# Group tags applied inside TensorE's sum, and a fence that sets non-neighbours apart, in a graph kernel on Trainium2

## The chip, the cores and the metric

The kernel runs on one core of one Trainium2 chip. The metric is the device time of one execution in microseconds (us). Before the change it is 3187.29 us, the median of 3 runs (3184.47 to 3189.19). Engines are named as in the profile: PE is TensorE's matmul, PEld its weight load, DVE is VectorE, ACT is ScalarE, POOL is GpSimd, SP is SyncE.

## The reference, cut to what matters

There are B = 16 graphs of N = 512 nodes with C = 64 features. Four graph layers follow each other; the change touches only the first. For every node it thins the neighbourhood, then takes three weighted quantiles of every feature over the neighbours that are left:

```python
neigh = (adj_ > 0) & ~eye
rank = jnp.cumsum(ni, axis=-1) - ni                 # the how-manieth neighbour of its row
nb = ni.sum(-1)
skip = jnp.maximum(jnp.where(nb > T, (nb + K - 1) // K, 1), 1)      # T, K = 10, 2
rem = neigh & (sk > 1) & (rank % sk == sk - 1) & mask[:, :, None]
rem = rem | jnp.swapaxes(rem, 1, 2)
adj_d = jnp.where(rem, 0.0, adj_)
s = jnp.sort(jnp.where(nd[..., None], x[:, None, :, :], jnp.inf), axis=2)
for tau, w in zip((0.25, 0.5, 0.75), (0.25, 0.5, 0.25)):
    pos = tau * jnp.maximum(nv - 1, 0); lo, hi = floor(pos), ceil(pos)
    agg += w * (s[lo] + (pos - lo) * (s[hi] - s[lo]))
```

The output is a layer norm of x plus the last layer, shape (16, 512, 64), float32.

## The kernel before, in words

**Staging.** At the start DVE makes tables in `stage`, SP stores them to memory (`consts_d`) and loads them back later as `consts`. All features of all graphs are then sorted at once by a network of comparisons on DVE; its swaps are replayed to give every node its rank in each feature. Graph 0's preparation is laid into this replay. Then comes the main loop over 16 graphs, and after it a loop for the last three layers that the change does not touch.

**The main loop is a pipeline of three graphs.** In one round, graph `b` is selected (`select`) and turned into indices (`bits_*` on DVE), graph `b + 1` (called `p` in `region`) is prepared, graph `l = b - 1` is looked up in `units` (48 units; in each, PE spreads indices into `bcast`, ACT makes `hot` of them, PE multiplies `hot` with a table into `rows`, ACT evicts `rows` into `prod`, PE adds up in `found_bank`), and graph `d = b - 2` runs its dense part. The order of all this on PE, ACT and DVE is written out by hand: the same `select` and `region` stand once per engine, with `units(l, STEP[n])` between the other pieces, so each engine works through its own list in order and waits on semaphores.

**Preparation of graph p**, in order: ACT converts the adjacency (`adj_b`), PE turns it, ACT keeps it (`neigh_t`), SP stores it; DVE waits for that store and clears the diagonal (`clear_own`, L1424); PE counts neighbours (L584); DVE works out for each node the place of its dropped neighbours (`middles`: `s1`, `s2`); PE counts up along each row with an upper triangle of ones (`count_up`, L594); ACT takes the distance from the middle (`apart_from`, L1001, `apart_of`); DVE compares with `s2` and multiplies by the adjacency (`drop`, L1445); PE adds both directions (`both_ways`, L604 to L607); ACT and DVE finish `kept_t`.

**Selection of graph b** goes over 4 tiles of 128 nodes. PE multiplies the kept adjacency with `member` in 8 chunks of 512 columns (`chunk`, L624): chunks 0 and 1 are counts, 2 to 5 two sets of bit words, 6 and 7 the plane `first` from which the first neighbour of the next group is read. ACT evicts them (L1046). DVE's `select(b, i, l)` then marks where each quantile's group starts (L1496) and what lies below (L1498), makes differences of words (L1501), masks the exponent of `first` (L1504), multiplies it by a tag that holds the group's number (L1505, `first_at`) and multiplies the starts by it (L1508). PE sums the result over 15 groups with the identity as weights (`sum_first`, L748). `tile_read` tells ACT after L1505 that words and `first` may be overwritten.

## Time and profile before

| | |
|---|---|
| median of 3 runs | 3187.29 us (3184.47 to 3189.19) |
| the profiled execution | 3195.59 us, of which span 3193.8 us |
| DVE busy | 2805.5 us, 88% |
| PE busy / weight loads | 2251.2 us, 70% / 1000.7 us, 31% |
| ACT busy | 1991.7 us, 62% |
| sort and replay | to about 520 us |
| main loop | about 520 to 2860 us |
| last layers | to the end |

Busy time is the time in which an engine has an instruction in work. Matmuls overlap, so a busy PE is not one at its peak, and a matmul's own duration is longer than the step to the next one: eight L594 matmuls take 1.19 us in the chain, though each has a duration of 0.2 to 0.4 us. The same holds on DVE to a smaller degree, where the next instruction starts some 0.08 us before the end of the last. PEclk is the granted clock of TensorE as a share of 2.4 GHz; it stands at 1.2 or at 2.4 GHz, and a share in a window is the mean of the two.

### The profile page before, as it was taken

What the parts mean: (1) busy time and instruction counts of PE and PEld (TensorE: products, weight loads), DVE (VectorE), ACT (ScalarE), POOL (GpSimd) and SP (SyncE); (2) the same over time, 40 slices, a digit from 0 to 9 for tenths busy, and PEclk for the clock granted to TensorE, in tenths of its full rate; (3) what the DMA queues carried; (4) which work ended last, traced back from release to release, by engine and by line L of the source; (5) the groups of instructions that cost most, each with busy time, mean ns of one, the idle gap of its engine ahead of it and who ended that gap; (6) DMA issues with size and microseconds to landing.
All of it is one profiled execution on the core that took longest, in us unless ns stands there. A gap on an engine that the chain in (4) does not pass through costs nothing.

```text
span 3193.8 us, 45583 instructions
## 1 busy us (share of the span) xinstructions
PE 2251.2 (70%) x16081; PEld 1000.7 (31%) x16234; DVE 2805.5 (88%) x5398; ACT 1991.7 (62%) x3077; POOL 12.4 (0%) x24
## 2 busy tenths in 40 slices
PE   0000014387888988888888988888898889776996
PEld 0000002232333333333333333333333333224674
DVE  7999998998999989899999999999898999545776
ACT  2111443278787887778788877878788877741322
POOL 0000000000000000000000000000000000000000
PEclk6555557688998989899999989899898989886777
DMA  3001000000101001010100101010100100000101
GB/s 68 0 0 26 31 0 0 22 24 11 37 8 34 13 29 33 10 33 12 36 11 31 21 21 33 12 37 9 32 15 27 34 10 19 10 20 27 40 26 40
DMA packets 126915, 72.05 MB, mean 23 GB/s; under 512 B 95512, under 2 KB 110058, under 8 KB 126698
## 3 DMA queue, kind: packets, MB, share of 16 engines
q1 hardware_dynamic: 122570, 68.23, 8.3%
q8 instruction: 121, 1.98, 0.3%
q10 hardware_dynamic: 4128, 1.05, 0.2%
q14 instruction: 96, 0.79, 0.1%
HBM read 41.05 MB, written 15.58 MB: 18 GB/s over the span
## 4 chain that ended last, share of the span: by engine, by line
PE 44%; DVE 32%; ACT 13%; issue 7%; SPq 2%; DMA 1%; DVEq 0%; ACTq 0%
PE ring L624 10%; PE rows L665 8%; ACT hot L1078 6%; PE bcast L637 5%; PE found_bank L677 5%; DVE keys L1326 3%; DVE keys L1327 3%; PE bcast L748 2%; PE bcast L757 2%; PE bank L919 2%; ACT prod L1071 2%; DVE picked L1524 2%; DVE delta L1367 2%; DVE delta L1365 1%; DVE perm L1369 1%
## 5 line engine op out<-in xcount | busy, mean ns | idle before, releaser
L1078 ACT ACTIVATE hot<-bcast,consts 128x1024 f16<-128x1024 f32 x744 | 830.7, 1117 | 136.0 <-PE bcast L637 135.5
L665 PE MATMUL rows<-hot,table 128*64 128x512 f16 x3072 | 525.7, 423 | 0.0
L624 PE MATMUL ring<-member,neigh_t 128*128 128x512 bf16 x1925 | 488.9, 392 | 40.0 <-issue 15.1
L1071 ACT ACTIVATE prod<-rows 128x512 f32<-128x512 f32 x720 | 431.1, 599 | 10.4 <-PE rows L665 10.4
L637 PE MATMUL bcast<-idx_t,consts 32*128 32x512 f16 x1488 | 311.3, 415 | 159.6 <-ACT hot L1078 158.0
L654 PE MATMUL rows<-fine_rows,consts 32*128 32x512 bf16 x768 | 316.3, 412 | 18.8 <-DMA fine_rows<-turned 18.1
L562 PE MATMUL ring<-identb,adj_b 128*128 128x128 bf16 x256 | 33.1, 258 | 368.9 <-ACT adj_b L974 357.6
L624 PEld LDWEIGHTS ring<-member,neigh_t 128*128 128x128 bf16 x2048 | 187.4, 101 | 318.8 <-issue 100.2
L677 PE MATMUL found_bank<-prod,consts 128*32 128x512 f32 x1536 | 240.2, 702 | 11.3 <-ACT prod L1071 10.5
L637 PEld LDWEIGHTS bcast<-idx_t,consts 32*128 32x128 f16 x1488 | 70.8, 92 | 499.0 <-ACT hot L1078 332.2
L1524 DVE TENSOR_TENSOR picked<-picked 128x3072 uint16<-128x3072 uint16 (+2 forms) x192 | 209.5, 1091 | 11.2
L1046 ACT ACTIVATE words<-ring 128x512 uint16<-128x512 f32 x256 | 153.4, 600 | 97.9 <-PE ring L624 79.4
L665 PEld LDWEIGHTS rows<-hot,table 128*64 128x64 f16 x3072 | 115.1, 112 | 190.6 <-issue 186.6
L968 ACT ACTIVATE keys<-keys 128x1024 f32<-128x1024 f32 (+7 forms) x72 | 35.5, 544 | 216.2 <-DVE keys L1327 216.2
L562 PEld LDWEIGHTS ring<-identb,adj_b 128*128 128x128 bf16 x256 | 19.6, 111 | 406.1 <-issue 332.7
L1014 ACT ACTIVATE swap<-swapped 128x2048 f16<-128x2048 uint8 (+8 forms) x45 | 73.8, 1643 | 111.5 <-DVE delta L1367 105.1
L1046 ACT ACTIVATE late<-ring 128x512 bf16<-128x512 f32 x128 | 76.9, 601 | 75.4 <-PE ring L624 73.3
L1516 DVE TENSOR_TENSOR picked<-below,words 128x2880 f16<-128x2880 bf16 x64 | 106.1, 1658 | 7.2
L1415 DVE TENSOR_TENSOR member<-words,shares 128x3072 bf16<-128x3072 bf16 x64 | 112.0, 1751 | 0.0
L1490 DVE TENSOR_TENSOR picked<-below,late 128x3072 uint16<-128x3072 bf16 x64 | 112.0, 1751 | 0.0
L1518 DVE TENSOR_TENSOR picked<-below,late 128x3072 uint16<-128x3072 bf16 x64 | 112.0, 1750 | 0.0
L1508 DVE TENSOR_TENSOR picked<-picked,first_at 128x2880 bf16<-128x2880 bf16 x64 | 106.1, 1658 | 2.2
(347 smaller groups left out, 4326.8 us busy)
## 6 DMA issues: line engine op xcount, KB each, us to landing
late<-in_adj_dram SPq DMA_DIRECT2D x16, 1024.0 KB, 5.4
adjt_d<-neigh_t SPq DMA_DIRECT2D x16, 512.0 KB, 2.7
fine_rows<-turned SPq DMA_DIRECT2D x512, 8.0 KB
fine_rows<-turned SPq DMA_DIRECT2D x512, 16.0 KB
turned<-adjt_d SPq DMA_DIRECT2D x16, 512.0 KB, 3.5
adj_s<-adjt_d SPq DMA_DIRECT2D x16, 512.0 KB, 3.8
xt_d<-keys SPq DMA_DIRECT2D x2, 1024.0 KB, 10.5
parts_d<-parts SPq DMA_DIRECT2D x4, 512.0 KB, 6.9
```

The lines of the kernel that those rows point to most:

```text
L624: ins = mm(ring[u % 2][:, :], kept_t[:, j, P * i:P * i + P], member[:, j, n // 2, 512 * (n % 2):512 * (n % 2) + 512], start=(j == 0), stop ...
L637: ins = mm(to[:, h, :], sel_a[r:r + 32, at:at + P], idx_t[r:r + 32, k, :], start=True, stop=True, tile_position=(r, 0))
L654: mm(rows[u % 2][:, :], sel_f[r:r + 32, :], fine_rows[r:r + 32, 2 * k + ROW_SLOT[g8], :], start=True, stop=False, tile_position=(r, 0), sk ...
L665: ins = mm(rows[u % 2][C * h:C * h + C, :], table[:, s, GROUPS * h + g8, :], hot[:, u % HOT, h, :], start=False, stop=(s == 1), skip_group ...
L677: mm(found_bank[to:to + 32, :], sum_to[:, g8 % 4, :], prod[:, u % DEEP, :], start=(m == 0), stop=(u >= UNITS - 4), skip_group_check=True). ...
L1046: run(dst, ring[u % 2][:, :], ACT.Copy).then_inc(S["cw_ev"], 1)
L1071: run(prod[:, u % DEEP, :], rows[u % 2][:, :], ACT.Relu).then_inc(S["prod_by_act"], 1)
L1078: run(hot[:, u % HOT].rearrange(flat), spread_bank(l, u)[0][:, 0:2, :].rearrange(flat), ACT.Relu, bias=eq_bias[:, :]).then_inc(S["hot_read ...
L1415: tt(member[:, j, 1:4, :].rearrange("p s (g c) -> p s g c", g=G), own[:, :, :].unsqueeze(1).to_broadcast([P, 3, G, C]), shares[:, :, j, :] ...
L1490: did(tt(picked[:, w], below[:, :], change[:, w, :].unsqueeze(1).to_broadcast([P, TAUS, G * C]), ALU.mult))
L1518: tt(picked[:, 2], below[:, :, :], change[:, 2, :].unsqueeze(1).to_broadcast([P, TAUS, G * C]), ALU.mult).then_inc(S["mask_used"], 1)
L1524: then(tt(a[:, :, 0:n], a[:, :, 0:n], a[:, :, n:2 * n], ALU.bitwise_xor))
```

## The change

Five things are done. (1) The 15 group tags no longer go into `first_at` on DVE; they are the weights of PE's sum: `tagged` holds 15 identities of 128 x 128, each scaled by its tag. L1505 goes, and L1508 reads the plane `first` itself. (2) ACT's leave to overwrite is told in two parts: `words_read` after the words are read, and `first_picked`, after L1508, for `first`. (3) In `count_up` a matmul of `adj_b` with `fence` (an identity times 4096) opens each of the 4 sums, so that neighbours carry 4096 more than non-neighbours; `s1` takes it off again. (4) `drop` is then one comparison with one scalar, without the product with `adj_b`. (5) At the start DVE makes `fence`, `tags` and `tagged`; the table `consts` grows by 448 columns of 4 bytes; one memset on POOL goes.

```diff
-FIELDS = (... ("group_id", 512, F16), ("first_tag", 512, BF16), 
+FIELDS = (... ("group_id", 512, F16), ("tagged", (G - 1) * 64, BF16),
...
             def count_up(b, i):
...
+                mm(ring[i % 2][:, :], fence[:, :], adj_b[:, i, :], start=True, stop=False)
                 for j in range(NT):
-                    ins = mm(ring[i % 2][:, P * j:N], neigh_t[:, j, P * i:P * i + P], upper[:, 0:N - P * j], start=(j == 0), stop=(j == NT - 1))
+                    ins = mm(ring[i % 2][:, P * j:N], neigh_t[:, j, P * i:P * i + P], upper[:, 0:N - P * j], start=False, stop=(j == NT - 1))
...
                 for g in range(G - 1):
-                    ins = mm(first_sum.rearrange("p (k c) -> p k c", k=TAUS), identb[:, :], plane[:, :, C * g:C * g + C], start=(g == 0), stop=(g == G - 2),
+                    ins = mm(first_sum.rearrange("p (k c) -> p k c", k=TAUS), tagged[:, g, :], plane[:, :, C * g:C * g + C], start=(g == 0), stop=(g == G - 2),
...
                 if n == 0:
-                    wait(act, S["tile_read"], NT * b + i - 1)
                     wait(act, S["cnt_read"], NT * b + i - 1)
                 if n == 2:
-                    wait(act, S["tile_read"], NT * b + i)
+                    wait(act, S["words_read"], NT * b + i)
+                if n == 6:
+                    wait(act, S["first_picked"], NT * b + i)
...
+            did(ts(fence[:, :], ident[:, :], FENCE, None, ALU.mult))
...
-            did(ts(made_of["first_tag"], made_of["group_id"], 1.0 / 32, 1.0 + 2.0 / 32, ALU.mult, ALU.add))
+            then(ts(tags, made_of["group_id"], 1.0 / 32, 1.0 + 2.0 / 32, ALU.mult, ALU.add))
+            did(tt(made_of["tagged"].rearrange("p (g n) -> p g n", n=P), ident[:, :].unsqueeze(1).to_broadcast([P, G - 1, P]),
+                   tags.rearrange("p (g c) -> p g c", c=C)[:, 1:, 0:1].to_broadcast([P, G - 1, P]), ALU.mult))
...
-                then(ts(s1, f1, -1.0, 1.0, ALU.mult, ALU.add))
+                then(ts(s1, f1, -1.0, 1.0 - FENCE, ALU.mult, ALU.add))
...
                 dve.wait_ge(S["apart_ready"], NT * b + i + 1)
-                stt(out=drop1[:, i, :], in0=apart_of[:, i % 2, :], scalar=s2[:, i:i + 1], in1=adj_b[:, i, :], op0=ALU.is_equal, op1=ALU.mult).then_inc(S["drop_ready"], 1)
+                ts(drop1[:, i, :], apart_of[:, i % 2, :], s2[:, i:i + 1], None, ALU.is_equal).then_inc(S["drop_ready"], 1)
...
-                did(v.tensor_copy(change[:, 1:3, last:], words[:, 1:3, 0:C]))
+                v.tensor_copy(change[:, 1:3, last:], words[:, 1:3, 0:C]).then_inc(S["words_read"], 1)
                 dve.wait_ge(S["cw_ev"], NT * CW * b + CW * i + CW)
                 then(ts(first[:, :].bitcast(U16), first[:, :].bitcast(U16), FIRST, None, ALU.bitwise_and))
-                tt(first_at[:, 0:last], first[:, C:], first_tag[:, 1:, :].rearrange(flat), ALU.mult).then_inc(S["tile_read"], 1)
-                dve.wait_ge(S["tile_read"], NT * b + i + 1)
-                need(count[0])
-                tt(starts[:, :, 0:last], starts[:, :, 0:last], first_at[:, 0:last].unsqueeze(1).to_broadcast([P, TAUS, last]), ALU.mult).then_inc(S["first_picked"], 1)
+                tt(starts[:, :, 0:last], starts[:, :, 0:last], first[:, C:].unsqueeze(1).to_broadcast([P, TAUS, last]), ALU.mult).then_inc(S["first_picked"], 1)
```

Here is PE in the main loop, at the first two of the four `count_up` of a graph; L637, L654 and L665 are one unit of the lookup. First before, then the changed kernel, whose line numbers are 2 higher from there on:

```order
L637 MATMUL bcast<-idx_t,consts 128x512 x2
L654 MATMUL rows<-fine_rows,consts 128x512
L665 MATMUL rows<-hot,table 64x512 x4
L594 MATMUL ring<-consts,neigh_t 128x512
L594 MATMUL ring<-consts,neigh_t 128x384
L594 MATMUL ring<-consts,neigh_t 128x256
L594 MATMUL ring<-consts,neigh_t 128x128
```

```order
L639 MATMUL bcast<-idx_t,consts 128x512 x2
L656 MATMUL rows<-fine_rows,consts 128x512
L667 MATMUL rows<-hot,table 64x512 x4
L594 MATMUL ring<-adj_b,fence 128x512
L596 MATMUL ring<-consts,neigh_t 128x512
L596 MATMUL ring<-consts,neigh_t 128x384
L596 MATMUL ring<-consts,neigh_t 128x256
L596 MATMUL ring<-consts,neigh_t 128x128
```

One matmul of 512 columns more stands in front of every count; nothing else moves on PE.

The second place is DVE in the selection of a tile, before and changed (L1504 is L1510 there, L1508 is L1511):

```order
L1502 COPY late<-words 128x2x64
L1504 TENSOR_SCALAR late<-late 128x1024 [waits cw_ev]
L1505 TENSOR_TENSOR first_at<-late,consts 128x960 [waits dve_chain]
L1508 TENSOR_TENSOR picked<-picked,first_at 128x3x960 [waits dve_chain,tile_read]
L1509 TENSOR_SCALAR words<-cnt 128x960
```

```order
L1508 COPY late<-words 128x2x64
L1510 TENSOR_SCALAR late<-late 128x1024 [waits cw_ev]
L1511 TENSOR_TENSOR picked<-picked,late 128x3x960 [waits dve_chain]
L1512 TENSOR_SCALAR words<-cnt 128x960
```

One instruction is gone per tile. The third place is ACT, at the eviction of the 8 chunks of a tile (cnt, words, late), before and changed:

```order
L1046 ACTIVATE cnt<-ring 128x512 [waits cw_ps,cnt_read,tile_read]
L1046 ACTIVATE cnt<-ring 128x512 [waits cw_ps]
L1046 ACTIVATE words<-ring 128x512 [waits cw_ps,tile_read]
L1046 ACTIVATE words<-ring 128x512 [waits cw_ps] x3
L1046 ACTIVATE late<-ring 128x512 [waits cw_ps] x2
```

```order
L1049 ACTIVATE cnt<-ring 128x512 [waits cw_ps,cnt_read]
L1049 ACTIVATE cnt<-ring 128x512 [waits cw_ps]
L1049 ACTIVATE words<-ring 128x512 [waits cw_ps,words_read]
L1049 ACTIVATE words<-ring 128x512 [waits cw_ps] x3
L1049 ACTIVATE late<-ring 128x512 [waits cw_ps,first_picked]
L1049 ACTIVATE late<-ring 128x512 [waits cw_ps]
```

The wait of the words comes loose from `first`, and the first `late` has a wait of its own.

## Rows read from the trace of the kernel before

**Rows 1.** The page: busy time of each engine, and the chain that ended last.

```profile
PE 2251.2 (70%) x16081; PEld 1000.7 (31%) x16234; DVE 2805.5 (88%) x5398; ACT 1991.7 (62%) x3077; POOL 12.4 (0%) x24
PE 44%; DVE 32%; ACT 13%; issue 7%; SPq 2%; DMA 1%; DVEq 0%; ACTq 0%
```

**Rows 2.** Timeline of DVE: start, us, clearing of the diagonal, idle before and releaser.

```profile
875.98 0.63 DVE L1424 TENSOR_TENSOR neigh_t<-neigh_t,identb 128x128 bf16<-128x128 bf16 x4 [1.39 <-DMA adjt_d<-neigh_t]
...
1304.03 0.63 DVE L1424 TENSOR_TENSOR neigh_t<-neigh_t,identb 128x128 bf16<-128x128 bf16 x4 [4.19 <-DMA adjt_d<-neigh_t]
...
1585.39 0.63 DVE L1424 TENSOR_TENSOR neigh_t<-neigh_t,identb 128x128 bf16<-128x128 bf16 x4
...
2577.20 0.63 DVE L1424 TENSOR_TENSOR neigh_t<-neigh_t,identb 128x128 bf16<-128x128 bf16 x4 [0.60 <-DMA adjt_d<-neigh_t]
```

**Rows 3.** Windows, one graph each: engines busy, PEclk, DMA share, GB/s.

```profile
1158.80:1304.00 145.20, 127.36 (x886) 51.78 (x896) 130.82 (x265) 113.26 (x179) 0.00 (x0) 0.88 0.09 23
1304.00:1445.40 141.40, 122.61 (x886) 49.73 (x896) 130.94 (x265) 112.95 (x179) 0.00 (x0) 0.91 0.09 23
1585.40:1725.00 139.60, 120.03 (x886) 49.30 (x896) 130.88 (x266) 113.04 (x178) 0.00 (x0) 0.93 0.09 24
```

**Rows 4.** Timeline of DVE in the selection of one tile.

```profile
1243.93 1.23 DVE L1496 TENSOR_SCALAR picked<-cnt,above 128x960 bf16<-128x960 f16 x3
1245.07 1.22 DVE L1498 TENSOR_SCALAR below<-cnt,limit 128x960 bf16<-128x960 f16 x3
...
1248.03 0.66 DVE L1505 TENSOR_TENSOR first_at<-late,consts 128x960 bf16<-128x960 bf16 x1
1248.72 1.66 DVE L1508 TENSOR_TENSOR picked<-picked,first_at 128x2880 bf16<-128x2880 bf16 x1
```

**Rows 5.** Timeline of DVE around the four drops of one graph.

```profile
1316.22 1.42 DVE L1445 SCALAR_TENSOR_TENSOR adj_b<-apart_of,small,adj_b 128x512 bf16<-128x512 f16 x2
1317.55 0.68 DVE L1412 TENSOR_TENSOR words<-group_of,consts 128x1024 bf16<-128x1024 f16 x1
...
1321.92 1.42 DVE L1445 SCALAR_TENSOR_TENSOR adj_b<-apart_of,small,adj_b 128x512 bf16<-128x512 f16 x2 [1.42 <-ACT apart_of L1001]
```

**Rows 6.** The chain in the same stretch: start, us, what.

```profile
1316.27 1.19 PE ring L594 x8
...
1321.31 0.59 ACT apart_of L1001
...
1321.92 1.43 DVE adj_b L1445 x2
...
1323.69 0.38 PE ring L605
```

**Rows 7.** Timeline of PE in the same stretch, behind the last drop.

```profile
1323.69 0.38 PE L605 MATMUL ring<-adj_b,minus 128*128 128x512 bf16 x1 [0.73 <-DVE adj_b L1445]
```

**Rows 8.** Timeline of ACT: lookups around the counts, and the second pair of distances.

```profile
1311.06 1.11 ACT L1078 ACTIVATE hot<-bcast,consts 128x1024 f16<-128x1024 f32 x1 [1.68 <-PE bcast L637]
...
1317.83 1.11 ACT L1078 ACTIVATE hot<-bcast,consts 128x1024 f16<-128x1024 f32 x1 [0.47 <-PE bcast L637]
...
1321.19 1.27 ACT L1001 ACTIVATE apart_of<-ring,small 128x512 f16<-128x512 f32 x2
```

**Rows 9.** The chain in the replay, the first round, and two later selections.

```profile
418.67 0.75 DVE adj_b L1445
...
428.10 0.74 DVE adj_b L1445
...
541.35 0.67 DVE first_at L1505
...
615.64 1.42 DVE adj_b L1445 x2
...
619.93 1.32 DVE adj_b L1445 x2
...
1500.51 0.67 DVE first_at L1505
...
1829.42 0.67 DVE first_at L1505
```

**Rows 10.** Timelines of DVE and SP at the start, and the DMA issues.

```profile
19.78 2.29 DVE L1325 TENSOR_TENSOR swapped<-keys 128x2048 uint8<-128x2048 f32 x1 [8.07 <-ACT keys L954]
...
33.39 2.29 DVE L1325 TENSOR_TENSOR swapped<-keys 128x2048 uint8<-128x2048 f32 x1 [6.91 <-DMA xt_d<-keys]
...
19.64 0.42 SPq L376 DMA_DIRECT2D consts_d<-parts  x1
20.10 2.07 SPq L379 DMA_DIRECT2D xt_d<-keys  x2
...
xt_d<-keys SPq DMA_DIRECT2D x2, 1024.0 KB, 10.5
consts_d<-parts SPq DMA_DIRECT2D x1, 881.0 KB, 3.8
```

**Rows 11.** Waits in total: engine, line, waited for, us, times, longest.

```profile
PEld bcast L748 <- DVE picked L1508: 14.0, 8, 10.0
```

More of the change, by code:

```diff
@@ L35 @@
 FIRST, TAG = 0x7F80, 0x7C
+FENCE = 4096.0
 DEEP = 6
@@ L47 @@
 TURN_ORDER = (K, 0, K + 1, K + 2, 1, 2, 3, 4, 5)
-FIELDS = (("sel_a", 256, F16), ("upper", 256, BF16), ("group_id", 512, F16), ("first_tag", 512, BF16),
+FIELDS = (("sel_a", 256, F16), ("upper", 256, BF16), ("group_id", 512, F16), ("tagged", (G - 1) * 64, BF16),
           ("sum_to", 4 * 32, F32), ("one_u", 32, U16), ("ones_b", 1, BF16), ("sel_f", 64, BF16), ("eq_bias", 1, F32))
@@ L161, in build @@
         minus = sb("minus", [P, P], BF16)
+        fence = sb("fence", [P, P], BF16)
         rowsum = sb("rowsum", [P, B, NT], F32)
@@ L227, in build @@
             at_f = stage[:, 4104:4112]
+            tags = stage[:, 4608:5120].bitcast(BF16)
             column, shift = delta[:, 0:512], swap[:, 0, 0:512]
@@ L242, in build @@
         upper, sel_a, sel_f, one_u, eq_bias = (views[n] for n in ("upper", "sel_a", "sel_f", "one_u", "eq_bias"))
-        group_id, first_tag = (views[n].rearrange("p (g c) -> p g c", c=C) for n in ("group_id", "first_tag"))
+        group_id, tagged = (views[n].rearrange("p (g c) -> p g c", c=w) for n, w in (("group_id", C), ("tagged", P)))
         sum_to = views["sum_to"].rearrange("p (g c) -> p g c", c=32)
@@ L251, in build @@
         adj_f = late[:, :, :].rearrange("p a n -> p (a n)").bitcast(F32).rearrange("p (t n) -> p t n", t=NT)
-        first_at = sb("first_at", [P, G * C], BF16)
         adj_b = sb("adj_b", [P, NT, N], BF16)
@@ L331, in build @@
             first_picked size_picked sums_ps sums_ev perm_made twos_done stage_ready stage_out consts_in neighT_ready nb_ps middle_ready apart_ready cnt_ps drop_ready rs_ps kept_made kept_ready nv_ps nv_read member_ready cw_ps cw_ev
-            tile_read cnt_read mask_used idx_ready idxT_ps idxT_ev table_in adjl_in bc_ps place_ps
-            odd_in later_in hot_ready row_ps prod_by_act prod_by_dve found_ps nb_read sum_ev xt_out span_ready unspan_clear unspan_in x_t_in x1T_ps x1T_ev gcn_ev h_ps h_ev y_ps z_ready
+            cnt_read mask_used idx_ready idxT_ps idxT_ev table_in adjl_in bc_ps place_ps
+            odd_in later_in words_read hot_ready row_ps prod_by_act prod_by_dve found_ps nb_read sum_ev xt_out span_ready unspan_clear unspan_in x_t_in x1T_ps x1T_ev gcn_ev h_ps h_ev y_ps z_ready
             sd_ready x1_ready tr_ps split_ready g_ps dve_chain out_done sp_passed pe_passed w23_ready wT_ps
@@ L509, in _ @@
             made(g.memset(below[:, :, (G - 1) * C:], 1.0))
-            made(g.memset(first_at[:, (G - 1) * C:], 0.0))
             made(g.memset(table[:, :, :, :], 0.0))
```

## The prediction

> **What bounds the kernel now.** I first read the page's busy times and its chain. DVE is busy 88% of the span, PE 70%, ACT 62%; but the chain that ended last lies 44% on PE and only 32% on DVE [rows 1], and much of DVE's share is the sort and its replay before 520 us. So DVE is the fullest engine and yet not clearly the one that sets the pace. Next I read the timeline of DVE at one fixed place of each round, the clearing of the diagonal: where DVE comes to it early, it waits for the store of the adjacency, which hangs on PE and ACT; where it comes late, it does not wait. Of the 14 clearings from 737 us on, 11 come with a wait of 0.3 to 4.2 us and 3 with none [rows 2]. From 876.0 to 2577.2 us lie 12 rounds, 141.8 us each on average [rows 2]. Then the windows of single rounds: DVE's busy time is 130.8 or 130.9 us in every round, whether the round takes 139.6, 141.4 or 145.2 us; what goes with the length is the granted clock, 0.93, 0.91, 0.88, and with it PE's busy time, 120.0, 122.6, 127.4 us [rows 3]. A round is thus paced by the PE-ACT loop, with DVE only 0 to 4 us behind it. The chain says the same: followed through the main loop, the 14 rounds from 660 us on have first_at on it 15 times out of 56 (first at 932 us, in four rounds, last at 1829.42) [rows 9]; elsewhere it runs over PE and ACT, touching DVE mainly at the clearing and at the second pair of drops, which is on it in every round [rows 6].
>
> How near the two are: by the clock shares, a round has 25.4 us at 1.2 GHz at 0.91 and 34.8 us at 0.88 (twice the missing share times the length), and 3.8 us more of length, 0.40 us for each us. From the 141.4 us round down to 0.93 (19.5 us) that gives 139.1 us for the PE-ACT loop alone, where DVE-paced rounds take 139.6 [rows 3]. The two ways differ by 0.5 us in 140.
>
> **The change part by part.**
>
> *first_at goes.* L1505 starts at 1248.03 and L1508 at 1248.72: 0.69 us per tile [rows 4], 64 tiles, 44 us of DVE. Where it is on the path: in the first selection, which has no lookups beside it, all 4 times [rows 9], so 4 x 0.69 = 2.8 us gained. In later rounds DVE merely reaches the clearing 2.8 us sooner and waits there longer; that wait is what is late next. What it can give there stands under "pacing" below.
>
> *The drop as one comparison.* Two old drops follow each other from 1316.22 to 1317.55, 0.665 us apiece [rows 5]. The new one is a comparison with one scalar like L1496, three of which (960 columns, float16 to bfloat16) take 1.14 us from start to start, 0.38 each [rows 4]. Bounds for 512 columns: 0.20 (by columns alone) and 0.38 (no cheaper than 960). I take 0.26, since most of the duration goes with the columns; the gain is 0.40 us each (0.28 to 0.46), 26 us of DVE in all. On the path: the 4 in the replay, where the chain is all DVE, and the 4 of the first round [rows 9]: 8 x 0.40 = 3.2 us. In the 14 later rounds the second pair is on the chain, but only half of it can be gained: its first drop starts at 1321.92 while the ACT pair that feeds both runs from 1321.19 to 1322.46 [rows 8]. The second drop cannot start before about 1322.55, so the pair ends at 1322.91 instead of 1323.34: 0.43 us. PE has waited 0.73 us for it [rows 7], so it can take it. 14 x 0.43 = 6.0 us.
>
> *The fence.* Four matmuls of 512 columns per graph. Eight L594 matmuls (two tiles, 2560 columns) took 1.19 us in the chain at the full clock [rows 6], 0.24 us per 512 columns; at 1.2 GHz twice that is the upper bound, zero the lower, where PE would have waited. PE is behind here, not ahead: ACT waits 1.68 us for PE's spread just before the first pair of counts and 0.47 us just after the second [rows 8], and both pairs are on the chain. So I take 0.24 x 4 = 0.95 us per round at full price, 14 rounds: +13.3 us. In the replay and the first round DVE is the path and the fence is free. Its weight load is hidden as those of the other counts are.
>
> *Tags as weights.* The 15 matmuls of a sum keep their number and size and had a weight load each before; only which weights changes. Nothing. Multiplying by `first` in place of `first_at` is the same form: nothing.
>
> *ACT's waits.* Words may be overwritten sooner. The new wait stands before chunk 6: behind it on ACT are the rest of the tile's evictions and the units, and PE waits for both. L1508 ends at 1250.4 us [rows 4]; ACT came to chunk 6 of the next tile about 7 us later. Nothing in the main loop. If this cover went, each of 60 tiles would pay up to the 1.66 us of L1508.
>
> *The start.* DVE makes `tagged`, 1920 columns of float32 with two tensors, at most the 2.29 us of a float32 operation of 2048 columns, and `fence`; it then waited 8.07 us for ACT, which hides both [rows 10]. The table is 224 KB longer. It is stored just ahead of the 2048 KB whose landing DVE waits for until 33.39 us, 6.91 us [rows 10]: 2929 KB from 19.64 us to there are 213 KB per us, so 1.05 us later (0 if the engines had room). I take +1.0.
>
> *Pacing.* Four rounds were wholly or partly paced by DVE. Freed from it they fall back to the PE-ACT loop, 0.5 us shorter each: 2 us. PE's weight loads waited 14.0 us for L1508 in 8 places, 10.0 of it in one at the start [rows 11]; the other 4.0 us, each under the 0.69 us by which L1508 comes sooner, would go. I count half, as PE had other work at hand in some: 2 us.
>
> *The sum.* -2.8 - 3.2 + 1.0 = -5.0 us before the first lookups; then -6.0 + 13.3 - 2 - 2 = +3.3 us. Together -1.7 us, on the profiled execution's 3195.6 us (span 3193.8 and 1.8 around it). That execution is 8 us above the median 3187.3; I take the difference as the same in both kernels, and the forecast is 3185.6, say 3186 us.
>
> The page says DVE is at 88%, and the Trainium skill ("Perfetto Trace Analysis", Identifying the Most-Contended Engine) says to take the engine of highest occupancy as the one to speed up first. By that rule the 70 us taken off DVE should come out almost whole. It is my first rival; the windows speak against it.
>
> **The rivals.**
>
> *A: DVE is the pace after all.* If every round followed DVE, it would give back 4 x (0.69 + 0.40) = 4.4 us: 15 rounds and the replay, 66 us, less the 1.0 of the start: about 3122 us. For it: 88%, and three clearings without a wait. Against it: equal DVE work in rounds 6 us apart in length [rows 3], and 11 clearings that waited. A milder form: half of it, 3155. Chance of both 0.12.
>
> *B: the clock gets better.* The rounds of 141.4 and 145.2 us have 6 to 15 us more at 1.2 GHz than those of 139.6 [rows 3]. The counts and PE's shorter wait for the drops make PE a little fuller. If with that every round came out like the best, the 12 rounds would average 139.1 + 0.95 - 0.43 = 139.6 in place of 141.8: 14 x 2.2 = 31 us, less the pacing gain already in it; with -5, 3154 us. Half of it is likelier: 3168. For it: three rounds in a row held 0.93. Against it: the low stretches lie where PE waits for the adjacency and at the turn of the rounds, not at the counts. Chance 0.20.
>
> *C: slower.* The fence is the only work added to the loop that sets the pace, and it moves every later piece of the round. DVE's pace of 139.6 us held four rounds steady at 0.93; with DVE early, nothing holds them, and they may fall to 0.91 like their neighbours. Place: the rounds from 1445 to 1865 us and the one at 907. Price: 4 x (141.4 - 139.6) = 7 us, and one further round in four going to 0.88, 3 x 3.8 = 11 us: 3186 + 18 = 3204 us. It decides from the point at which the freed rounds show 0.91 or less. For it: PE-paced rounds are the longer ones in this trace. Chance 0.20.
>
> *D: the change buys DVE less than it says* (the comparison runs no faster than the product, 0.66 us). Then -3.2 and -6.0 go: 3195 us. Against it: the form L1496. Chance 0.03.
>
> **How the numbers follow.** The forecast has 0.45, with 3179 to 3193 as its own range. Of measurement: within 0.2% (6.4 us, 3180.9 to 3193.7) nothing can be told from no change. Faster: all of A, 0.17 of B's 0.20 and 0.06 of the forecast's: 0.35. Slower: 0.17 of C, 0.02 of D, 0.03 of the forecast: 0.22. The rest, 0.43, is no change. The range of 8 in 10 goes down to B's milder form and a little beyond, and up to C: 3160 to 3203. It takes in the fence at nothing (-13) and at double (+13).
>
> **What would show it.** After the change: no L1505; drops of 0.26 us from start to start; DVE busy about 2735 us; the wait at the clearing longer by 2.5 to 3 us in most rounds and present in all; PE's wait before L605 shorter by about 0.4 us or a new one of DVE on ACT between the drops of the second pair; rounds of PE-paced length 0.5 us up at the same clock; the first lookups (about 650 us) 5 us sooner; DVE's share of the chain below 25%. The forecast is wrong if the rounds shorten by more than 2 us with an unchanged clock (A), or if the mean clock of the rounds moves by more than 0.01 (B or C).

## The result and the profile after

| | before | after |
|---|---|---|
| median (lowest to highest), 8 runs each | 3188.11 us (3184.47 to 3192.8) | 3198.93 us (3194.62 to 3205.38) |
| ratio | | 1.0028, 95% interval 1.0018 to 1.0039 |
| the profiled execution, its span | 3195.59 us, 3193.8 us | 3198.18 us, 3196.4 us |

The changed kernel is slower by 0.28%, some 9 us (the two medians are 10.8 us apart). The forecast was no change (3186 us, 1.7 us faster) with a range of 3160 to 3203; the time lies in the range, the sign was wrong. The first place to look is again the page, busy time and chain, of the changed kernel (before: [rows 1]):

```profile
PE 2270.3 (71%) x16145; PEld 1008.6 (32%) x16298; DVE 2741.5 (86%) x5336; ACT 1990.4 (62%) x3077; POOL 12.3 (0%) x23
PE 52%; DVE 21%; ACT 16%; issue 7%; SPq 2%; DMA 2%; DVEq 0%; ACTq 0%
```

DVE lost 64 us of work and 62 instructions, PE gained 64 matmuls and 19 us. DVE's share of the chain fell from 32% to 21%, and what it gave up went to PE. The clearing of the diagonal is the marker of the rounds; here it is in the changed kernel, on the timeline of DVE (start, duration, at the end the idle time before it and what ended that):

```profile
603.83 0.63 DVE L1430 TENSOR_TENSOR neigh_t<-neigh_t,identb 128x128 bf16<-128x128 bf16 x4
...
729.79 0.63 DVE L1430 TENSOR_TENSOR neigh_t<-neigh_t,identb 128x128 bf16<-128x128 bf16 x4 [0.25 <-DMA adjt_d<-neigh_t]
...
867.41 0.63 DVE L1430 TENSOR_TENSOR neigh_t<-neigh_t,identb 128x128 bf16<-128x128 bf16 x4 [2.87 <-DMA adjt_d<-neigh_t]
...
1295.78 0.63 DVE L1430 TENSOR_TENSOR neigh_t<-neigh_t,identb 128x128 bf16<-128x128 bf16 x4 [7.50 <-DMA adjt_d<-neigh_t]
...
1863.65 0.63 DVE L1430 TENSOR_TENSOR neigh_t<-neigh_t,identb 128x128 bf16<-128x128 bf16 x4 [2.30 <-DMA adjt_d<-neigh_t]
...
2579.81 0.63 DVE L1430 TENSOR_TENSOR neigh_t<-neigh_t,identb 128x128 bf16<-128x128 bf16 x4 [2.72 <-DMA adjt_d<-neigh_t]
```

The same places before, as far as [rows 2] do not have them:

```profile
607.46 0.63 DVE L1424 TENSOR_TENSOR neigh_t<-neigh_t,identb 128x128 bf16<-128x128 bf16 x4
...
737.02 0.63 DVE L1424 TENSOR_TENSOR neigh_t<-neigh_t,identb 128x128 bf16<-128x128 bf16 x4 [0.99 <-DMA adjt_d<-neigh_t]
```

The changed kernel is 3.6 us ahead at the first of them, 7.2 at the second and 8.6 at the third (867.41 against 875.98 [rows 2]). From there 12 rounds take 1712.4 us in place of 1701.2; it loses 11.2 us and is 2.6 us behind at 2577, which is the whole difference of the spans. So there are two parts: a start that gains, and rounds that lose 0.93 us each. The windows of single rounds and of the 12 together, after (for the rounds before, [rows 3]):

```profile
1150.90:1296.30 145.40, 127.92 (x890) 52.17 (x900) 126.70 (x262) 112.94 (x178) 0.00 (x0) 0.88 0.09 23
1296.30:1438.20 141.90, 123.60 (x890) 50.15 (x900) 126.81 (x262) 112.97 (x178) 0.00 (x0) 0.91 0.09 23
1723.80:1864.20 140.40, 121.41 (x890) 49.62 (x900) 126.81 (x263) 112.94 (x178) 0.00 (x0) 0.93 0.10 24
867.90:2580.30 1712.40, 1489.19 (x10684) 605.93 (x10800) 1521.65 (x3134) 1357.33 (x2138) 0.00 (x0) 0.91 0.09 23
```

and the 12 rounds before, in the same columns:

```profile
876.00:2577.20 1701.20, 1473.67 (x10636) 599.41 (x10752) 1570.76 (x3181) 1358.31 (x2138) 0.00 (x0) 0.91 0.09 23
```

DVE has 4.1 us less work in every round, as forecast. Rounds at the same granted clock, 0.88, 0.91 and 0.93, take 145.4, 141.9 and 140.4 us where [rows 3] have 145.2, 141.4 and 139.6: a cost of 0.2 to 0.8 us at an unchanged clock. The last of these pairs sets a round paced by PE and ACT against one that DVE paced.

**One round followed on ACT.** The rounds that begin at 1304.0 (before) and 1295.8 (after) run at the same clock, so their events can be laid side by side. ACT's lookups and the pair of distances, after:

```profile
1302.93 1.11 ACT L1081 ACTIVATE hot<-bcast,consts 128x1024 f16<-128x1024 f32 x1 [1.80 <-PE bcast L639]
...
1306.50 1.11 ACT L1081 ACTIVATE hot<-bcast,consts 128x1024 f16<-128x1024 f32 x1 [0.67 <-PE bcast L639]
...
1310.61 1.11 ACT L1081 ACTIVATE hot<-bcast,consts 128x1024 f16<-128x1024 f32 x1 [0.90 <-PE bcast L639]
...
1313.97 1.27 ACT L1003 ACTIVATE apart_of<-ring,small 128x512 f16<-128x512 f32 x2
```

Counted from the clearing, the first of these comes 7.15 us in (before 1311.06 - 1304.03 = 7.03 [rows 2, 8]) and the third 14.83 us in (before 13.80 [rows 8]). Across the two pairs of counts ACT falls back from 0.12 to 1.03 us; its waits for PE's spread grew from 1.68 to 1.80 and from 0.47 to 0.90 us. After the last drop it is at 0.54, and so it stays to the end of the round. The forecast for this was +0.95 for four fences and -0.43 for the pair of drops, +0.52. The drops themselves, timeline of DVE:

```profile
1308.38 0.62 DVE L1451 TENSOR_SCALAR adj_b<-apart_of,small 128x512 bf16<-128x512 f16 x2
1308.91 0.69 DVE L1418 TENSOR_TENSOR words<-group_of,consts 128x1024 bf16<-128x1024 f16 x1
...
1314.69 0.35 DVE L1451 TENSOR_SCALAR adj_b<-apart_of,small 128x512 bf16<-128x512 f16 x1 [2.82 <-ACT apart_of L1003]
1315.27 0.35 DVE L1451 TENSOR_SCALAR adj_b<-apart_of,small 128x512 bf16<-128x512 f16 x1 [0.23 <-ACT apart_of L1003]
```

Two take 0.53 us, 0.265 each, against 0.665 [rows 5]. The second pair is now split by a wait for ACT of 0.23 us, and PE finds it ready (before, 0.73 us of wait for `adj_b` [rows 7]):

```profile
1304.18 0.38 PE L594 MATMUL ring<-adj_b,fence 128*128 128x512 bf16 x1
...
1315.98 0.38 PE L607 MATMUL ring<-adj_b,minus 128*128 128x512 bf16 x1 [0.25 <-issue]
```

What the chain of waits has at this place (start, us, what):

```profile
1308.62 0.32 PE ring L594
1308.94 0.54 PE ring L596 x4
1309.48 0.22 PE ring L594
1309.70 0.54 PE ring L596 x4
...
1314.08 1.16 ACT apart_of L1003 x2
...
1315.23 0.01 ACT hot L1081
```

The fence is two links of it, and the drops are no link any more ([rows 6] had them with 1.43 us). Over the 14 rounds from 737 us on, the chain has the fence 42 times, three of its four matmuls in every round, and a drop once, at 747.22. The waits in total (who, for what, us, times, longest) tell where DVE's saved time went:

```profile
DVE neigh_t L1430 <- DMA adjt_d<-neigh_t: 48.4, 14, 7.5
DVE adj_b L1451 <- ACT apart_of L1003: 43.4, 29, 4.8
```

Before they were 15.9 us in 11 places and 19.8 us in 14. Of the 64 us of work taken off DVE, 56 came back as these two waits.

### The profile page after: what moved, and what is told of

It is laid out like the page before. It is cut to its first block, busy times and chain, and to the rows that moved or that the text cites. A ratio compares the mean times of both kernels' runs of the same rounds, so it can differ in the third digit from the quotient of the medians.

```text
span 3196.4 us, 45647 instructions
## 1 busy us (share of the span) xinstructions
PE 2270.3 (71%) x16145; PEld 1008.6 (32%) x16298; DVE 2741.5 (86%) x5336; ACT 1990.4 (62%) x3077; POOL 12.3 (0%) x23
## 4 chain that ended last, share of the span: by engine, by line
PE 52%; DVE 21%; ACT 16%; issue 7%; SPq 2%; DMA 2%; DVEq 0%; ACTq 0%
PE ring L626 13%; PE rows L667 9%; ACT hot L1081 7%; PE bcast L639 6%; PE found_bank L679 6%; DVE keys L1332 3%; DVE keys L1333 3%; PE bcast L750 3%; PE bcast L759 2%; ACT prod L1074 2%; PE bank L921 2%; DVE delta L1373 2%; DVE delta L1371 1%; DVE perm L1375 1%; DVE perm L1376 1%
## 5 line engine op out<-in xcount | busy, mean ns | idle before, releaser
L1081 ACT ACTIVATE hot<-bcast,consts 128x1024 f16<-128x1024 f32 x744 | 830.8, 1117 | 143.6 <-PE bcast L639 143.3
L656 PE MATMUL rows<-fine_rows,consts 32*128 32x512 bf16 x768 | 316.4, 412 | 16.2 <-DMA fine_rows<-turned 15.9
L679 PE MATMUL found_bank<-prod,consts 128*32 128x512 f32 x1536 | 240.1, 702 | 11.2 <-ACT prod L1074 10.4
L1527 DVE TENSOR_TENSOR picked<-picked 128x3072 uint16<-128x3072 uint16 (+2 forms) x192 | 209.5, 1091 | 11.2
L1511 DVE TENSOR_TENSOR picked<-picked,late 128x2880 bf16<-128x2880 bf16 x64 | 106.1, 1658 | 2.2
```

The costliest lines, as they stand in the source:

```text
L656: mm(rows[u % 2][:, :], sel_f[r:r + 32, :], fine_rows[r:r + 32, 2 * k + ROW_SLOT[g8], :], start=True, stop=False, tile_position=(r, 0), sk ...
L679: mm(found_bank[to:to + 32, :], sum_to[:, g8 % 4, :], prod[:, u % DEEP, :], start=(m == 0), stop=(u >= UNITS - 4), skip_group_check=True). ...
L1081: run(hot[:, u % HOT].rearrange(flat), spread_bank(l, u)[0][:, 0:2, :].rearrange(flat), ACT.Relu, bias=eq_bias[:, :]).then_inc(S["hot_read ...
L1527: then(tt(a[:, :, 0:n], a[:, :, 0:n], a[:, :, n:2 * n], ALU.bitwise_xor))
```

## Experiments

Two theories were to be told apart. The first: the rounds are the PE-ACT loop, the change is a sum of small terms of work (fence dear, drops cheap, tags nothing), and DVE's work in the rounds is free. The second: the work matters little, and what moved is the granted clock, because rounds that DVE no longer paces fall to a lower one. Beside them stand the old rivals: the fence is hidden in waits of PE, and DVE is the pace.

One thing had to be settled first. Executions of one and the same kernel differ in their mean granted clock, and their time with it: of one comparison's runs of the kernel before, one had 0.820 and took 3184.9 us, another 0.811 and took 3209.5. Over the 161 executions of the first three comparisons whose clock is known, each taken against the mean of its kernel, the time falls by 2.2 us for each 0.001 of mean clock (2.24 over all 190). The table gives, beside the measured ratio, the mean time taken at 0.817 with this slope (in brackets 95%). That is an adjustment and not a measurement, and it cannot say whether a kernel itself causes its clock.

| kernel | comparison | ratio to before (95%) | median us (runs) | mean clock | at 0.817, us |
|---|---|---|---|---|---|
| before | 2nd, 3rd, 4th | | 3195.4 (35), 3193.6 (29), 3203.1 (9) | .8154, .8163, .8123 | 3193.2 (0.6) |
| after_again | 3rd | 1.0022 (1.0012 to 1.0032) | 3202.5 | .8149 | 3196.5 (1.2), with the first 8 |
| before_again | 3rd | 0.9996 (0.9986 to 1.0007) | 3193.07 (12) | .8170 | 3192.9 (1.1) |
| tags_only | 2nd | 0.9977 (0.9963 to 0.9991) | 3187.21 (12) | .8187 | 3191.4 (1.1) |
| fence_only | 2nd | 1.0009 (0.9995 to 1.0023) | 3200.39 (12) | .8161 | 3197.7 (1.1) |
| fence_mm_alone | 2nd | 1.0014 (0.9999 to 1.0029) | 3200.63 (12) | .8187 | 3205.3 (0.9) |
| free_fence | 2nd | 0.9973 (0.9955 to 0.9992) | 3187.48 (12) | .8153 | 3183.3 (1.1) |
| no_fence_mm | 3rd | 0.9982 (0.9969 to 0.9996) | 3187.45 (12) | .8149 | 3184.5 (1.7) |
| ballast | 3rd | 1.0060 (1.0044 to 1.0075) | 3210.57 (5) | .8160 | 3210.4 (1.3) |
| free_fence_again | 4th | 0.9960 (0.9947 to 0.9974) | 3190.03 (5) | .8134 | 3183.0 (1.5) |
| free_fence_alone | 4th | 0.9955 (0.9941 to 0.9968) | 3188.27 (5) | .8148 | 3183.0 (0.9) |
| ff_pad1 | 4th | 0.9947 (0.9933 to 0.9961) | 3186.40 (5) | .8178 | 3187.6 (1.2) |
| ff_pad2 | 4th | 0.9959 (0.9946 to 0.9973) | 3189.89 (5) | .8168 | 3189.5 (0.4) |

Ratios of different comparisons should be held against each other with care: the kernel before itself stood at 3188, 3195, 3194 and 3203 us in the four, the last two of them on the same chip.

### tags_only: the tags moved into the sum, counts and drops as before

```diff
 (to the changed kernel)
-                mm(ring[i % 2][:, :], fence[:, :], adj_b[:, i, :], start=True, stop=False)
-                then(ts(s1, f1, -1.0, 1.0 - FENCE, ALU.mult, ALU.add))
+                then(ts(s1, f1, -1.0, 1.0, ALU.mult, ALU.add))
-                ts(drop1[:, i, :], apart_of[:, i % 2, :], s2[:, i:i + 1], None, ALU.is_equal)
+                stt(out=drop1[:, i, :], in0=apart_of[:, i % 2, :], scalar=s2[:, i:i + 1], in1=adj_b[:, i, :], op0=ALU.is_equal, op1=ALU.mult)
```

> The tags go into the sum and the product on DVE goes, but the drops are made as before and there is no fence. Theory 1 (a round is paced by PE and ACT; work on their path counts, DVE's does not): -2.8 us in the first selection, +1.0 at the start, nothing per round: 3186 us, 2 below before. Theory 2 (DVE's pace held several rounds at a high granted clock, and whatever makes DVE early loses that): 5 us more, 3191 us, with fewer rounds of 139.6 to 140 us than before. Rival (DVE sets the pace after all): 44 us faster, 3145 us.

It is faster than before, by 0.23%. Of that only 1.8 us (3193.2 - 3191.4) is there at equal clock, though 44 us of DVE work are gone (64 x 0.69 us from start to start; its busy time fell by 38.5 us): DVE is not the pace. The windows of this kernel, the 12 rounds and one that DVE had paced before, with the clearings at both its ends:

```profile
872.10:2571.90 1699.80, 1474.63 (x10639) 597.22 (x10756) 1540.23 (x3133) 1357.52 (x2138) 0.00 (x0) 0.91 0.09 23
1580.40:1722.00 141.60, 122.72 (x886) 49.70 (x896) 128.45 (x263) 112.89 (x179) 0.00 (x0) 0.91 0.09 23
```

```profile
1580.29 0.63 DVE L1429 TENSOR_TENSOR neigh_t<-neigh_t,identb 128x128 bf16<-128x128 bf16 x4 [3.35 <-DMA adjt_d<-neigh_t]
...
1721.85 0.63 DVE L1429 TENSOR_TENSOR neigh_t<-neigh_t,identb 128x128 bf16<-128x128 bf16 x4 [2.94 <-DMA adjt_d<-neigh_t]
```

With DVE out of the way the round that took 139.6 us at 0.93 [rows 3] takes 141.6 at 0.91. That is what the second theory said of this round. But the rounds that were at 0.88 are gone too: all 12 lie between 141.3 and 142.1 us, their sum of 1699.8 us is near the 1701.2 of before, and the kernel's mean clock is the highest of all, 0.8187. So DVE's pace is not needed to keep the clock up over the whole run.

### fence_mm_alone: before, with four matmuls more per graph that add nothing

```diff
 (to the kernel before)
+                mm(ring[i % 2][:, :], fence[:, :], adj_b[:, i, :], start=True, stop=False)    # fence is all zeros
-                    ins = mm(ring[i % 2][:, P * j:N], ..., start=(j == 0), stop=(j == NT - 1))
+                    ins = mm(ring[i % 2][:, P * j:N], ..., start=False, stop=(j == NT - 1))
```

> The kernel before with 4 more matmuls of 512 columns per graph in front of the counts, of a zero matrix; DVE does exactly what it did. This prices the matmul. Theory 1: 14 x 0.95 = +13 us, 3201 us, a little less where DVE paced the round. Theory 2: the same or less, since DVE is no earlier. Rival (DVE sets the pace): nothing, 3188 us.

The ratio, 1.0014, says little: the interval reaches from 0.9999 to 1.0029. The kernel ran at 0.8187 where the kernel before had 0.8154. At equal clock it costs 3205.3 - 3193.2 = 12.1 us, where 13.3 were forecast.

### fence_only: before, with the fence and the one comparison

```diff
 (to fence_mm_alone)
-FENCE = 0.0
+FENCE = 4096.0
-                then(ts(s1, f1, -1.0, 1.0, ALU.mult, ALU.add))
+                then(ts(s1, f1, -1.0, 1.0 - FENCE, ALU.mult, ALU.add))
-                stt(out=drop1[:, i, :], ..., op0=ALU.is_equal, op1=ALU.mult)
+                ts(drop1[:, i, :], apart_of[:, i % 2, :], s2[:, i:i + 1], None, ALU.is_equal)
```

> The fence matmul and the drop as one comparison, tags as before. Theory 1: each of 14 rounds +0.95 us for the fence and -0.43 for the drops, -3.2 us before the first lookups: +4, 3192 us. Theory 2: 5 us on top, 3197 us. Rival (DVE sets the pace): 26 us of DVE saved, 3162 us.

Not told from before by its ratio (0.9995 to 1.0023). Against fence_mm_alone it is 7.6 us faster at equal clock: that is what the cheaper drops are worth. Against the changed kernel, which has the tags besides, it is 1.2 us slower, within the error of both.

### free_fence: the changed kernel with the fence in the triangle's diagonal

The triangle of ones already meets each node's own adjacency block in the count. If its diagonal holds 4096, every neighbour carries the fence and no matmul is needed.

```diff
 (to the changed kernel)
-                mm(ring[i % 2][:, :], fence[:, :], adj_b[:, i, :], start=True, stop=False)
-            did(ts(made_of["upper"], place[:, :], own_p, None, ALU.is_ge))
+            then(ts(made_of["upper"], place[:, :], own_p, None, ALU.is_ge))
+            did(stt(out=made_of["upper"][:, 0:P], in0=ident[:, :], scalar=FENCE, in1=made_of["upper"][:, 0:P], op0=ALU.mult, op1=ALU.max))
-                then(ts(s1, f1, -1.0, 1.0 - FENCE, ALU.mult, ALU.add))
+                then(ts(s1, f1, -1.0, 2.0 - FENCE, ALU.mult, ALU.add))
```

> The whole change, but the 4096 comes without a matmul: the diagonal of the triangle that count_up multiplies with is 4096 in place of 1, and s1 takes 4095 off. PE then does what it did before the change, DVE what it does after. Theory 1: the 13.3 us of the fence go against the changed kernel: 3199 - 13 = 3186 us, or -5.0 and 14 x -0.43 against before: 3177 us; I expect between these, 3181. Theory 2: 5 us above theory 1's 3177, 3182 us at best and no DVE-paced rounds. Rival (DVE sets the pace): 3120 us.

Faster than before, 0.9973 (0.9955 to 0.9992), and 13.2 us below the changed kernel at equal clock: the fence again, measured by taking it away. Its windows, the slowest and the quickest round:

```profile
1439.20:1587.10 147.90, 130.52 (x886) 52.23 (x896) 126.82 (x262) 113.05 (x179) 0.00 (x0) 0.84 0.09 22
...
1868.00:2008.00 140.00, 120.54 (x886) 49.45 (x896) 126.84 (x263) 112.79 (x179) 0.00 (x0) 0.93 0.10 24
```

One kernel, the same work in both rounds (DVE 126.8 us, ACT 113), and 7.9 us between them. The better one, at 0.93 and with DVE early, takes 140.0 us: no less than the 139.6 of the DVE-paced rounds before [rows 3].

### before_again and after_again: both kernels a second time

No edit.

> The kernel before, as a variant of itself, for a second trace and for the noise of the comparison: ratio 1.000. Theory 1: its rounds fall into other patterns of clock than in the first trace. Theory 2: rounds paced by DVE (no wait at the clearing) again come with 20 to 21 us at 1.2 GHz, and the others with 25 or more.

> The changed kernel once more, next to the kernel before and the other variants. Fitted over all executions so far, the time falls by 2.1 us for each 0.001 of mean granted clock, and at an equal mean clock of 0.817 the kernels stand at 3193.1 (before), 3196.1 (changed), 3191.3 (tags only), 3197.8 (fence only), 3205.2 (matmul alone), 3183.4 (fence without a matmul). Theory 1 (the work on PE's path decides, the clock's share differs from one occasion to the next): 3 us above before at an equal clock again, whatever the medians do. Theory 2 (the change itself lowers the clock because DVE no longer paces any round): the mean clock is again lower than that of before, by 0.001 to 0.003, and the median 8 to 11 us above.

before_again is what it should be, 0.9996 (0.9986 to 1.0007); it shows how far a kernel compared with itself strays from 1. after_again repeats the verdict, 1.0022 (1.0012 to 1.0032). The 12 rounds of before_again and, below, of after_again:

```profile
875.30:2572.20 1696.90, 1466.23 (x10639) 596.86 (x10756) 1570.75 (x3180) 1358.33 (x2139) 0.00 (x0) 0.91 0.09 23
```

```profile
874.10:2585.80 1711.70, 1485.26 (x10687) 604.72 (x10804) 1521.31 (x3132) 1358.50 (x2139) 0.00 (x0) 0.91 0.09 23
```

Two executions of before are 4.3 us apart over the 12 rounds, at equal work. The difference between the kernels is 14.8 us here and 11.2 in the first pair of traces.

### no_fence_mm: the changed kernel, fence matmul and offset left out

```diff
 (to the changed kernel)
-                mm(ring[i % 2][:, :], fence[:, :], adj_b[:, i, :], start=True, stop=False)
-                then(ts(s1, f1, -1.0, 1.0 - FENCE, ALU.mult, ALU.add))
+                then(ts(s1, f1, -1.0, 1.0, ALU.mult, ALU.add))
```

> The changed kernel without the fence matmul and with the old offset; non-neighbours are not set apart, so this leaves out part of the selection of drops, and is run for its time alone. It should time like the variant whose triangle carries the 4096: theory 1: 3183 us at a mean clock of 0.817, 13 below the changed kernel. Rival (the matmul is hidden by PE's waits): no difference from the changed kernel.

12.0 us below the changed kernel at equal clock, 0.9982 to before. Here the adjustment can be done without: after_again ran in the same comparison at the same mean clock, 0.8149, and the mean times of the two, 3201.4 and 3189.0 us, are 12.4 us apart as measured. It agrees with free_fence, so the diagonal is no dearer than leaving the fence out.

### ballast: the changed kernel with one more operation of 1.16 us on DVE in every tile

```diff
 (to the changed kernel, between L1510 and L1511)
+                did(tt(picked[:, 1, 0:2, 0:last].bitcast(BF16), below[:, 0:2, 0:last], below[:, 0:2, 0:last], ALU.max))
```

> The changed kernel with one more DVE operation per tile whose result nobody reads (1920 columns of two tensors, 1.1 us), so that DVE has as much work per round as before the change. Theory 1: +4.3 us in the first selection, nothing in the rounds: 3200 us at a mean clock of 0.817. Theory 2: DVE paces rounds again, the clock rises by 0.001 to 0.003, and the median is not above that of the changed kernel. Rival (DVE sets the pace): 4.3 x 16 = 69 us slower, 3268 us.

The result of the added instruction is not read. The page of this kernel:

```profile
PE 2262.7 (71%) x16145; PEld 1006.5 (31%) x16298; DVE 2809.2 (88%) x5400; ACT 1990.6 (62%) x3077; POOL 12.3 (0%) x23
```

DVE is back at the 88% of before, and this time it costs: 1.0060, at equal clock 13.9 us more than after. About 4.3 us of this is the first selection, which has no cover: 4 x 1.07, the step from the added instruction to the next. The rest is in rounds like this one (its window, then DVE's timeline: the clearing at its start, the second pair of drops, the start of the first two selected tiles, and the clearing at its end):

```profile
1876.80:2020.40 143.60, 124.33 (x890) 50.85 (x900) 131.01 (x266) 112.77 (x178) 0.00 (x0) 0.90 0.09 23
```

```profile
1876.72 0.63 DVE L1430 TENSOR_TENSOR neigh_t<-neigh_t,identb 128x128 bf16<-128x128 bf16 x4
...
1894.95 0.35 DVE L1451 TENSOR_SCALAR adj_b<-apart_of,small 128x512 bf16<-128x512 f16 x1 [2.56 <-ACT apart_of L1003]
...
1927.86 1.23 DVE L1502 TENSOR_SCALAR picked<-cnt,above 128x960 bf16<-128x960 f16 x3 [0.28 <-DVE x_all L1676]
...
1944.76 1.23 DVE L1502 TENSOR_SCALAR picked<-cnt,above 128x960 bf16<-128x960 f16 x3
...
2020.28 0.63 DVE L1430 TENSOR_TENSOR neigh_t<-neigh_t,identb 128x128 bf16<-128x128 bf16 x4 [1.97 <-DMA adjt_d<-neigh_t]
```

and the selection in the DVE-paced round before that starts at 1585.39 [rows 2]:

```profile
1635.99 1.23 DVE L1496 TENSOR_SCALAR picked<-cnt,above 128x960 bf16<-128x960 f16 x3 [0.28 <-DVE x_all L1672]
...
1652.51 1.23 DVE L1496 TENSOR_SCALAR picked<-cnt,above 128x960 bf16<-128x960 f16 x3
```

The first clearing does not wait, so DVE comes late to it; yet 131.0 us of DVE work, as much as in [rows 3], make 143.6 us here and 139.6 there. The 4.0 us lie in three places. Up to the first selected tile it is 0.5 us (51.14 from the clearing against 50.60): DVE waits 2.56 us for ACT at the second pair of drops, so what the cheaper drops save is not gained. In the four tiles it is 1.5 us (16.90 for each against 16.52): the added operation is longer than the product that went. At the end it is 1.97 us of wait for the store of the adjacency, which has come later too. Equal work in sum is thus not equal work at the place where DVE is the pace. And DVE's pace did not hold the clock up: 9 of this kernel's 14 clearings come without a wait, and none of the 12 rounds from 874 us on is above 0.92. The margin of DVE in the changed kernel is smaller than the 2.3 to 7.5 us of its waits at the clearing of these rounds: 67.7 us more work in all cost 14.

### free_fence_again, ff_pad1, ff_pad2: the price of one matmul

```diff
 (to free_fence; ff_pad2 has i < 2)
+                if i < 1:
+                    mm(ring[i % 2][:, :], none[:, :], adj_b[:, i, :], start=True, stop=False)    # none is all zeros
```

> The whole change with the 4096 in the triangle's diagonal, once more, next to three neighbours. Theory 1 (work on PE's path, plus a share of the clock that each kernel's timing brings): ratio to before 0.997 again; at a mean clock of 0.817 it stands at 3183 to 3184 us against 3193 for before, and its rounds again alternate between 140 us and 148 us.

> The free fence with one matmul of 512 zero columns per graph put back, in front of the first count. Theory 1: +0.24 us in each of 14 rounds, +3.4 us at an equal clock: 3187 us at 0.817. What it does to the clock I can not forecast: if the share at 1.2 GHz is set by where the rounds fall against the clock's steps, a quarter of a microsecond more per round can move the mean clock by 0.002 to 0.004 either way, and the median by up to 8 us, more than the work it adds.

> The free fence with two matmuls of 512 zero columns per graph, in front of the first and second count. Theory 1: +6.7 us at an equal clock, 3190 us at 0.817; the median is not bound to lie above that of the variant with one matmul, since the clock's share moves on its own. Rival (time follows the work alone): medians rise evenly, by 3.4 us for each matmul.

The question was whether the cost of the fence grows with the number of matmuls or jumps with the clock. By medians it does neither: 3190.0, 3186.4 and 3189.9 us, with intervals that overlap. At equal clock it grows, from 3183.2 (both free_fence runs together) by 4.4 us for one, 6.3 for two and 13.3 for four (the changed kernel): about 3.3 per matmul and graph, over 14 rounds 0.24 us each.

### free_fence_alone: before, with the one comparison and the diagonal, tags as before

```diff
 (to the kernel before)
+            did(stt(out=made_of["upper"][:, 0:P], in0=ident[:, :], scalar=FENCE, in1=made_of["upper"][:, 0:P], op0=ALU.mult, op1=ALU.max))
+                then(ts(s1, f1, -1.0, 2.0 - FENCE, ALU.mult, ALU.add))
+                ts(drop1[:, i, :], apart_of[:, i % 2, :], s2[:, i:i + 1], None, ALU.is_equal)
```

> The kernel before with only the drop as one comparison and the 4096 in the triangle; tags on DVE as before. Theory 1: the tags are worth 1.8 us, so 3185 us at a mean clock of 0.817, 8 below before. Rival (DVE's time counts once PE is relieved): 3190 us or more, with rounds whose clearing does not wait.

0.9955 (0.9941 to 0.9968). At equal clock it is 10.2 us below before and even with free_fence: the drops are the whole gain, and the runs show nothing that moving the tags adds to it. The two kernels that carry the fence in the diagonal and add no matmul, with the tags moved (free_fence) or not (this one), are the quickest at equal clock of those that do the whole task; the runs do not tell which of the two is better. (tags_only, ff_pad1 and ff_pad2 also have ratios below 1.)

## Why the prediction was wrong

- **What bounds the kernel: right.** The rounds are the PE-ACT loop. 44 us less on DVE gave 1.8 us (tags_only), and the 64 us of the change came back as waits of DVE. Rival A, DVE as the pace, is refuted: less DVE work buys almost nothing, though ballast shows that more of it is not free. The Trainium skill's rule ("Perfetto Trace Analysis", Identifying the Most-Contended Engine), by which the engine of highest occupancy is the one to optimize first, does not hold here: DVE had 88%, and 44 us less on it alone gave 1.8 us.
- **The start: right.** -5.0 us were forecast before the first lookups, and the first of them comes 5.2 us sooner (timeline of ACT, before and after):

```profile
653.44 1.14 ACT L1078 ACTIVATE hot<-bcast,consts 128x1024 f16<-128x1024 f32 x1
```

```profile
648.21 1.14 ACT L1081 ACTIVATE hot<-bcast,consts 128x1024 f16<-128x1024 f32 x1
```

  At the clearing near 730 us it is 7.2 us and at the next 8.6; what came on top was not followed, and in the second traces the gain at the last of these places is only 1.3 us (875.5 against 874.2). The longer table delays the comparison that waits for the load behind it by 0.83 us (33.39 [rows 10]), where +1.0 was taken; timeline of DVE, after:

```profile
34.22 2.29 DVE L1331 TENSOR_TENSOR swapped<-keys 128x2048 uint8<-128x2048 f32 x1 [7.73 <-DMA xt_d<-keys]
```

- **The drop: right.** 0.265 us (0.26 forecast); the second pair is bound by ACT, as said. Worth -7.6 and -10.2 us at equal clock in two kernels, with -9.2 forecast (-3.2 and -6.0).
- **The fence: right.** 12.1, 13.2 and 12.0 us at equal clock (12.4 without adjustment), 13.3 forecast. Next to nothing of it is hidden: three of its four matmuls are on the chain in every round.
- **The tags: right in size, not proved.** -1.8, -1.2 and +0.2 us in three pairs of kernels, with -1.8 forecast (-2.8 and +1.0); each has an error of 1 to 2 us, and the last shows nothing.
- **Pacing: wrong, 4 us.** The step that failed is "freed from it they fall back to the PE-ACT loop, 0.5 us shorter each: 2 us", with the 139.1 us behind it, and with it the 2 us for PE's waits on L1508. Not one of the 12 rounds of tags_only, where only DVE's work changed, is below 141.3 us; of free_fence the best is 140.0 at 0.93. The 139.1 was a line through two rounds of other clocks, carried on past the last of them. The PE-ACT loop at 0.93 is no quicker than DVE's pace was, so nothing was to be had by freeing it. The waits of PE's weight loads on L1508 went as forecast, from 14.0 us in 8 places [rows 11] to 11.1 us in 2 (waits in total, after: PEld on L1511), but no time came of it: either PE had other work there, or the time went again into the next wait for ACT; which of these, was not tried.
- **The clock: counted at nothing, 4 to 6 us.** The forecast took the 8 us of the profiled execution above the median, and with them the clock, as the same in both kernels. Work without the pacing terms sums to -5.0 + 7.3 = +2.3 us; at equal clock +3.3 (1.3) is measured. The change measured is +9 us in the first comparison and +7 in the second. In the second the two kernels' mean clocks are .8149 and .8163, by the slope 3.1 us of it; the first has no clocks of its runs of before but that of the profiled one (0.816 at 3195.59 us). In the traces the 12 rounds lose 11.2 us, of which 12 x 0.52 = 6.2 are work. Time at 1.2 GHz is 26.0 us per round before and 26.9 after, 24.8 and 26.3 in the second traces. The slope, 2.2 us for 0.001 or 6.4 us at the lower clock, prices each of these us at 0.34, so they make 3.8 us of the first 11.2 and 6.1 of the second 14.8; with the 6.2 of work, 1.2 and 2.5 us are left over. That is an estimate from the slope, and no run sets the clock by itself.
- **Rival C: its event came, its reason is not shown.** After the change no round is paced by DVE, and of the three freed in a row, from 1438 us on, the first two take 142.0 and 143.6 us; the third keeps 0.93 and 140.4. (The prediction's "four rounds steady at 0.93" were three, from 1445 to 1865 us; the fourth round with L1505 on the chain, from 876 us, took 141.4 us at 0.91.) But tags_only and fence_mm_alone have the highest clocks of all, the first without a DVE-paced round, and ballast, with most of its rounds paced by DVE, has 0.8160. Why a kernel gets a mean clock of 0.815 or of 0.819 stays open: more work did not go with less clock (ff_pad1 has more than free_fence), and the kernel before itself was at .8123 to .8163 on different occasions.

Of the signs of the mechanism listed, all were there: no L1505, the first lookups 5.2 us sooner, DVE busy 2741.5 us (about 2735 forecast), waits at all 14 clearings and longer by 2.3 us on average ((48.4 - 15.9) / 14; 2.5 to 3 forecast), rounds up by half a microsecond, DVE at 21% of the chain (under 25%). Of the two signs of being wrong neither came: the rounds did not shorten, and the mean clock of the 12 rounds moved by 0.003 and, in the second traces, 0.005, where 0.01 was asked for (26.0 to 26.9 us of 142 at 1.2 GHz is 0.003). They were too coarse for a difference of 9 us. With both pacing terms out, the same sum gives +2.3 us and still "no change"; the sign was lost to 4 us of a hoped-for gain and about as much of clock, each smaller than the 6.4 us that separate the cases.

## What to carry to other kernels

Where two engines are near balance, price an edit by the chain at its fixed place in the loop, not by how full the engine is: four times 0.24 us per round put on the looping engines cost 12 to 13 us over the run, and four times 1.0 us taken off the fullest one gave 10 back (free_fence against before, at equal clock). Before a helper matmul is added to make an elementwise step cheaper, look whether a constant that is already multiplied there can carry it; here one diagonal did, and it turned a loss of 0.3% into a gain of 0.3 to 0.5%. And do not extrapolate a round's length beyond the best round seen: the line did not hold.

## What the runs showed of the hardware

Rounds of equal work differ with the granted clock by more than any edit here makes in a round: 140.0 us at 0.93 and 147.9 at 0.84 within one execution of free_fence. Mean clocks of single executions ran from 0.809 to 0.821 for the kernel before, with 2.2 us per 0.001 over all kernels, and whole occasions differed by 15 us (medians 3188 to 3203). Two kernels had nearly the same ratio to before, 1.0009 and 1.0014, and were 7.6 us apart at equal clock. For effects under 0.5% the clock of every run is to be read with its time.
